# Last stage of a fused two-layer block: one reciprocal root for two norms, bank-wise output copies, earlier signals, filler matmuls and a split store

## The reference

```python
x = x + W_o(softmax(q k^T / sqrt(16)) v)       # L1_xattn over 4096 context rows
x = x + L1_attn(layernorm(x))                  # 16 heads of 64, causal, z.reshape(b, s, h*dh) @ proj
X = layernorm(x)                               # eps 1e-5
nx = X * rsqrt(mean(X*X) + 1e-6) * g1          # RMS norm right behind it
X1 = X + attn(nx Wq, nx Wkc, nx Wvc) @ Wo      # 4 heads, shared keys and values
nx2 = rmsnorm(X1, g2)
logits = nx2 @ Wr.T + expert_bias              # 8 experts, the best two are weighted
moe = swiglu_shared(nx2) + sum_e combine[:, e] * swiglu_e(nx2)
x = x + (X1 + moe)
```

## Time and profile before

| | us |
|---|---|
| median of 3 runs | 748.99 (747.96 to 749.51) |
| the profiled execution | 750.28 |
| its span in the trace | 748.6 |
| PE busy | 646.4 (86%) |
| ACT busy | 464.5 (62%) |
| DVE busy | 413.4 (55%) |
| granted PE clock, mean | 0.963 of full |

### The profile page before, as it was taken

The page is one execution under the profiler, slowest core; times in us unless marked ns, Lnnn a source line. Parts: engine busy times, 40 slices in busy tenths (PEclk is TensorE's granted clock), DMA queues, the critical chain, the costliest instruction groups (busy, mean ns, idle before and its releaser), DMA issues. The chain is left out here.

```text
span 748.6 us, 14468 instructions
## 1 busy us (share of the span) xinstructions
PE 646.4 (86%) x4972; PEld 390.7 (52%) x4972; DVE 413.4 (55%) x903; ACT 464.5 (62%) x558; POOL 71.9 (10%) x148
## 2 busy tenths in 40 slices
PE   1698777878788769898589999999999899988997
PEld 1354444444445345575235555555555567754886
DVE  6576352231322315865578898988883426446443
ACT  3899969999999974472036676767767046303100
POOL 3010201000100003000110101111110200000000
PEclk9999979999999999999758999999999999999899
DMA  5787765384433114000802332323230740000000
GB/s 132 217 245 212 232 205 168 105 239 152 143 112 109 49 25 151 1 1 0 287 9 72 86 81 76 88 79 84 77 83 2 241 139 1 2 0 1 0 1 14
DMA packets 52694, 73.39 MB, mean 98 GB/s; under 512 B 10866, under 2 KB 29618, under 8 KB 52658
## 3 DMA queue, kind: packets, MB, share of 16 engines
q1 hardware_dynamic: 51890, 72.19, 33.0%
q10 hardware_dynamic: 768, 0.73, 0.3%
HBM read 58.89 MB, written 12.85 MB: 96 GB/s over the span
## 5 line engine op out<-in xcount | busy, mean ns | idle before, releaser
L1575 DVE TENSOR_REDUCE sb_m_blk<-ps 128x1 f32<-128x512 f32 x256 | 159.6, 683 | 22.8 <-PE ps L1432 21.7
L1383 ACT ACTIVATE sb_probs<-ps 128x1024 f32<-128x1024 f32 x128 | 125.9, 1025 | 52.9 <-PE ps L1462 51.7
L651 ACT ACTIVATE sb_probs<-ps 128x1024 f32<-128x1024 f32 x128 | 124.0, 1016 | 16.5 <-PE ps L697 14.2
L655 ACT ACTIVATE sb_probs<-sb_probs,sb_neg_cap,sb_cap 128x4096 f32<-128x4096 f32 x32 | 121.6, 3801 | 1.1
L714 PE MATMUL ps<-sb_probs,sb_v_st 128*32 128x256 f32 x1024 | 77.5, 400 | 41.1 <-ACT sb_probs L655 38.7
L1432 PE MATMUL ps<-sb_k_st,sb_q_m 96*128 96x512 bf16 x256 | 91.4, 402 | 2.7 <-DVE sb_m_blk L1575 2.0
L697 PE MATMUL ps<-sb_q_st,sb_k_st 112*128 112x256 bf16 x512 | 76.6, 285 | 5.9 <-DMA sb_k_st<-k_parts_l 4.2
L1462 PE MATMUL ps<-sb_q_st,sb_k_st 115*128 115x256 bf16 x512 | 77.7, 275 | 1.4 <-ACT sb_probs L1383 1.4
L697 PEld LDWEIGHTS ps<-sb_q_st,sb_k_st 112*128 112x128 bf16 x512 | 46.2, 101 | 49.7 <-ACT sb_probs L651 23.8
L1478 PE MATMUL ps<-sb_probs,sb_v_st 128*32 128x256 f32 x1024 | 67.7, 385 | 0.2 <-ACT sb_probs L1383 0.2
L714 PEld LDWEIGHTS ps<-sb_probs,sb_v_st 128*32 128x32 f32 x1024 | 24.2, 110 | 70.4 <-ACT sb_probs L655 49.3
(11 more groups left out here) (264 smaller groups left out, 875.0 us busy)
## 6 DMA issues: line engine op xcount, KB each, us to landing
sb_k_st<-k_parts_l SPq DMA_DIRECT2D x223, 64.0 KB, 2.0
sb_k_st<-k_parts_l SPq DMA_DIRECT2D x93, 128.0 KB, 3.2
k_parts_l<-sb_v_proj SPq DMA_DIRECT2D x24, 256.0 KB
k_parts_l<-sb_early SPq DMA_DIRECT2D x48, 128.0 KB
sb_v_proj<-ctxT_blocks SPq DMA_DIRECT2D x8, 512.0 KB, 8.9
sb_early<-ctxT SPq DMA_DIRECT2D x7, 512.0 KB, 4.0
sb_v_rows<-ctx_by_pair SPq DMA_DIRECT2D x7, 512.0 KB, 3.9
sb_k_st<-k_parts_l SPq DMA_DIRECT2D x64, 32.0 KB, 1.8
```

Of the source, the lines that this page charges most:

```text
L651: a.activation(probs[:, j % 2, 4 * g:4 * g + 4, :], scores_bank(g), ACT.Tanh).then_inc(s["tanh"], 1)
L655: a.activation(probs[:, j % 2], probs[:, j % 2], ACT.Exp, bias=k.neg_cap[:, 0:1], scale=k.cap[:, 0:1]).then_inc(s["exp"], 1)
L1383: sc.activation(probs[:, g], scores_bank(g), ACT.Exp).then_inc(s["exp"], 1)
L1575: v.tensor_reduce(k.m_blk[:, b, q, blk:blk + 1], k.ps[:, m_bank(m_turn_of(idx)), :], AX.X, ALU.max).then_inc(s["m_read"], 1)
```

## The change

- `keep_busy` gets a number of columns; one call of 256 columns (`D`) is added behind the transposes in `update_pe` with `turn=True` (two places), and around the last `sel` of `stage_cross1`.
- `small_dve` calls `beside(n)` at the end of each pair; in the causal attention this copies bank 4, 5 and 6 behind pairs 5, 9 and 13; bank 7 is copied at the end. The first half of the projection waits for two of these copies, the second for all four. The two calls of filler ahead of it are gone.
- The two roots become one ahead of the first use: with variance s of the rows and layer norm scale 1/sqrt(s + 1e-5), the product of both norms' scales is 1/sqrt(s(1 + 1e-6) + 1e-11). `k.xn` is written straight from `k.x`; the layer-normed rows `k.x_ffn` are made later, behind the g1 scaling, with a root of their own. Fillers there go from nine calls to four and one of half width.
- The key product comes first and signals alone, then queries, then values.
- `expert_bias` is loaded to all 128 partitions and added by DVE in place of a copy; the two L1789 products go.
- The last expert's two row tiles go to banks 6 and 7, each with a signal of its own, and `k.x` is stored in two transfers, one for each row tile.

```diff
-    k.f_be = fs[0:1, 1428:1436]
+    k.f_be = fs[:, 1428:1436]
...
+def bn_moments(k, link, src):
 
     v = k.nc.vector
     link(*[v.bn_stats(k.ln_stats[:, t, :], src[:, t, :]) for t in range(QT)])
     link(*[v.bn_aggr(k.ln_mv[:, t, :], k.ln_stats[:, t, :]) for t in range(QT)])
...
-def keep_busy(k, n, bank):
+def keep_busy(k, n, bank, cols=2 * D):
 
     for _ in range(n):
-        k.nc.tensor.matmul(k.ps[:, bank, :], k.ones_sq[:, :], k.w1_o[:, :, :].rearrange("p t n -> p (t n)"), start=True, stop=True)
+        k.nc.tensor.matmul(k.ps[:, bank, 0:cols], k.ones_sq[:, :], k.w1_o[:, :, :].rearrange("p t n -> p (t n)")[:, 0:cols], start=True, stop=True)
...
     if turn:
         transpose_rows(k, k.o_nat, 0, k.sem(tag + "_oT_ps"))
+        keep_busy(k, 1, 3, D)
...
+        if beside is not None:
+            beside(n)
...
+                keep_busy(k, 1, 2, D)
                 sel(H - 1, 1, n_m * H, H - 1)
+                keep_busy(k, 1, 2, D)
...
-    sp.dma_start(k.f_be, i["L1_ffn_expert_bias"].unsqueeze(0)).then_inc(done, 16)
+    sp.dma_start(k.f_be, i["L1_ffn_expert_bias"].unsqueeze(0).to_broadcast([P, N_EXP])).then_inc(done, 16)
...
+    def out_bank(n, q):
+        return 6 + q if n == N_EXP else 4 + n % 2
...
-            sp.wait_ge(k.sem("f_x"), 2 * (N_EXP + 1))
-            sp.dma_start(k.out.rearrange("a (t p) d -> p (a t) d", p=P), k.x[:, :, :]).then_inc(k.sem("out"), 16)
-            sp.wait_ge(k.sem("out"), 16)
+            for q in range(QT):
+                sp.wait_ge(k.sem("f_x"), QT * N_EXP + q + 1)
+                sp.dma_start(k.out.rearrange("a (t p) d -> p (a t) d", p=P)[:, q, :], k.x[:, q, :]).then_inc(k.sem("out"), 16)
+            sp.wait_ge(k.sem("out"), 16 * QT)
...
-            keep_busy(k, 2, 0)
-            pe.wait_ge(k.sem("e_oT"), 1)
-
-
             for q in range(QT):
+                pe.wait_ge(k.sem("e_oT"), 2 * (q + 1))
...
-            keep_busy(k, 9, 0)
+            keep_busy(k, 4, 0)
+            keep_busy(k, 1, 0, D)
...
+            for c in range(KT):
+                last = t.matmul(k.ps[:, 5, 0:S], k.f_wkc[:, c, :], k.xnT[:, c, :], start=(c == 0), stop=(c == KT - 1))
+            last.then_inc(k.sem("f_proj"), 1)
...
-                    t.matmul(o, k.xnT[:, c, q * P:(q + 1) * P], k.f_wr[:, c, :], start=(c == 0), stop=False)
-                last = t.matmul(o, k.ones_row[0:1, 0:P], k.f_be, start=False, stop=True)
+                    last = t.matmul(o, k.xnT[:, c, q * P:(q + 1) * P], k.f_wr[:, c, :], start=(c == 0), stop=(c == KT - 1))
...
+                    if q == 1 or n == N_EXP:
+                        last.then_inc(k.sem("g_rows"), 1)
...
-            v.tensor_copy(k.e_oT.rearrange("p (b g) i c -> p b (g i c)", b=4), k.ps[:, 4:8, :]).then_inc(k.sem("e_oT"), 1)
+            def copy_out(bank):
+                dve.wait_ge(k.sem("small_out"), causal.base + 4 * (bank + 1))
+                v.tensor_copy(k.e_oT.rearrange("p (b g) i c -> p b (g i c)", b=4)[:, bank, :], k.ps[:, 4 + bank, :]).then_inc(k.sem("e_oT"), 1)
+
+            def beside(n):
+                if n % 4 == 1 and n > 4:
+                    copy_out(n // 4 - 1)
+
+            small_dve(k, dve, causal, beside)
+            copy_out(3)
...
-            layer_norm(k, dve, link, k.x, k.x_ffn, k.sem("f_x0"))
-            dve.wait_ge(k.sem("f_x0"), QT)
-            rms_norm(k, dve, link, k.x_ffn, k.sem("f_xn"))
+            bn_moments(k, link, k.x)
+            link(v.tensor_scalar(k.rs_v[:, 0:QT], k.ln_mv[:, :, 1], 1.0 + 1e-6, 1e-5 * 1e-6, ALU.mult, ALU.add))
+            rsqrt(k, link, QT)
+            for q in range(QT):
+                v.tensor_scalar(k.xn[:, q, :], k.x[:, q, :], k.ln_mv[:, q, 0:1], k.rs_y[:, q:q + 1], ALU.subtract, ALU.mult).then_inc(k.sem("f_xn"), 1)
             dve.wait_ge(k.sem("f_w_in"), 16 * 9)
             weigh_turned(k, dve, 0, k.sem("f_xnT_ps"), k.sem("f_xnT"))
-            dve.wait_ge(k.sem("f_proj"), 1)
+            link(v.tensor_scalar(k.rs_v[:, 0:QT], k.ln_mv[:, :, 1], 1e-5, None, ALU.add))
+            rsqrt(k, link, QT)
+            link(*[v.tensor_scalar(k.x_ffn[:, q, :], k.x[:, q, :], k.ln_mv[:, q, 0:1], k.rs_y[:, q:q + 1], ALU.subtract, ALU.mult)
+                   for q in range(QT)])
+            dve.wait_ge(k.sem("f_proj"), 2)
...
+                    if q == 1 and n == N_EXP:
+                        dve.wait_ge(k.sem("g_rows"), n + 2)
```

More of the change, by code:

```diff
@@ L249, in allocate @@
     k.oT_pad = flat(k.v_st[:, :, :, :], "b c n")[:, 0:1024].rearrange("p (g q) -> p g q", g=4)
-def norm_moments(k, link, src):
+def bn_moments(k, link, src):
     v = k.nc.vector
@@ L256, in norm_moments @@
     link(*[v.bn_aggr(k.ln_mv[:, t, :], k.ln_stats[:, t, :]) for t in range(QT)])
+def norm_moments(k, link, src):
+    v = k.nc.vector
+    bn_moments(k, link, src)
     link(v.tensor_scalar(k.rs_v[:, 0:QT], k.ln_mv[:, :, 1], 1e-5, None, ALU.add))
@@ L1057, in small_act, with small_dve @@
     copy_turned(len(a.pairs) - 1)
-def small_dve(k, dve, a):
+def small_dve(k, dve, a, beside=None):
     v = k.nc.vector
@@ L1643, in load_late_weights @@
         sp.dma_start(k.f_g[:, n, :], i[f"L1_ffn_g{n + 1}_cols"]).then_inc(done, 16)
-    sp.dma_start(k.f_be, i["L1_ffn_expert_bias"].unsqueeze(0)).then_inc(done, 16)
+    sp.dma_start(k.f_be, i["L1_ffn_expert_bias"].unsqueeze(0).to_broadcast([P, N_EXP])).then_inc(done, 16)
 def rms_norm(k, dve, link, src, done):
     v = k.nc.vector
-    link(*[v.bn_stats(k.ln_stats[:, t, :], src[:, t, :]) for t in range(QT)])
-    link(*[v.bn_aggr(k.ln_mv[:, t, :], k.ln_stats[:, t, :]) for t in range(QT)])
+    bn_moments(k, link, src)
     link(v.tensor_tensor(k.rs_t[:, 0:QT], k.ln_mv[:, :, 0], k.ln_mv[:, :, 0], ALU.mult))
@@ L1764, in _ @@
             pe.wait_ge(k.sem("f_w_in"), 16 * 9)
+            for c in range(KT):
+                last = t.matmul(k.ps[:, 5, 0:S], k.f_wkc[:, c, :], k.xnT[:, c, :], start=(c == 0), stop=(c == KT - 1))
+            last.then_inc(k.sem("f_proj"), 1)
             for m in range(KT):
                 for c in range(KT):
[L1767 to L1770, removed]
+                    last = t.matmul(k.ps[:, 3, m * S:(m + 1) * S], k.f_wq[:, c, m * P:(m + 1) * P], k.xnT[:, c, :],
+                                    start=(c == 0), stop=(c == KT - 1))
+            last.then_inc(k.sem("f_proj"), 1)
             for m in range(KT):
@@ L1809, in down @@
                     pe.wait_ge(k.sem("f_x"), 2 * (n - 1))
-                rows_linear(k, k.f_hT[:, n % 2], KT, k.f_exp[experts[n]][2], None, 4 + n % 2, k.sem("g_rows"))
+                for q in range(QT):
+                    for c in range(KT):
+                        last = t.matmul(k.ps[:, out_bank(n, q), q * D:(q + 1) * D], k.f_hT[:, n % 2, c, q * P:(q + 1) * P],
+                                        k.f_exp[experts[n]][2][:, c, :], start=(c == 0), stop=(c == KT - 1))
+                    if q == 1 or n == N_EXP:
+                        last.then_inc(k.sem("g_rows"), 1)
             hidden(0)
@@ L1944, in _ @@
                 for q in range(QT):
-                    v.scalar_tensor_tensor(out=k.x[:, q, :], in0=k.ps[:, 4 + n % 2, q * D:(q + 1) * D],
+                    if q == 1 and n == N_EXP:
+                        dve.wait_ge(k.sem("g_rows"), n + 2)
+                    v.scalar_tensor_tensor(out=k.x[:, q, :], in0=k.ps[:, out_bank(n, q), q * D:(q + 1) * D],
                                            scalar=k.f_comb[:, q, experts[n]:experts[n] + 1], in1=k.x[:, q, :],
```

6 lines of the change are left out of this document (3 added, 3 removed).

## The result

| | before | after |
|---|---|---|
| median, us | 748.76 (747.96 to 749.51, 4 runs) | 740.53 (736.70 to 742.25, 4 runs) |
| profiled execution, us | 750.28 | 741.15 |
| span, us | 748.6 | 739.4 |
| granted PE clock, mean | 0.963 | 0.967 |

The ratio is 0.988, 95% interval 0.985 to 0.992: 8.2 us faster, where 9.6 was forecast. In the profiled pair the difference is 9.1 us.

The account below looks back on a forecast made before the run. PE was taken to bound the attention and experts, with latencies between them; gains 1.19 + 3.45 + 0.81 + 0.83 + 1.4 + 1.5 + 0.45 = 9.63 us from 748.99 gave 739.4, own range 738.2 to 741.

Parts of the forecast that it names:

- Copy by bank: Causal attention to projection: 2.42 us gained at the end, 1.23 lost to copies in the loop, net 1.19 (0.35 to 2.1).
- One root: Residual update to transposes in stage_self1: one joint root shortens the path by 3.45 us; the moved DVE work is covered.
- Signals: Latent attention's products to scores: keys, queries and values signalled singly gain 0.81 us (0.4 to 0.85).
- Border fillers: Border ahead of stage_self1: three half-width fillers hold the clock for the output product, gain 1.4 us, other bound 0.
- The router: Router to first expert instructions: a shorter clock dip gains 1.5 us (0 to 3.0), four PE bias instructions fewer gain 0.83.
- bias products: At the router, four PE instructions go as DVE adds the bias: 0.83 us, partly at the low clock.
- the dip lasts half as long: Router's low clock: thin stretch cut from 3.7 to 2.9 us, middle case taken, gain 1.5 us of a 3.0 us cost.
- Store: End of kernel: two transfers, the last issued 0.40 us earlier and landing 0.05 sooner, gain 0.45 us (0.2 to 0.6).
- the clock that doesn't follow: Rival: both dips, at the stage_self1 border and the router, stay; gain 6.73 us, 742.3 us; chance 0.24.
- The clock that follows fully: Rival: router dip vanishes, 737.9 us, or 736.5 with the dip at 280.7 gone too; chance 0.16.
- The copies that eat their gain: Rival in the causal attention: three copies cost 0.69 us each, term 0.35 or below, 740.2 us; inside the forecast's own range.
- The slower one: Rival: shortened fillers let the clock stay low through the latent attention up to the experts, +12 us, 754; chance 0.03.

Follow-up runs that it names:

- One copy: Changed kernel with the four bank copies undone: one copy of 2048 columns behind the causal attention, with filler and one wait as before; median 739.06 us.
- norm alone: Kernel before with only the joint root, the second root behind the g1 scaling and five filler calls for nine; 746.64 us against 749.91, 0.997.
- no border fillers: Changed kernel without its three half-width fillers between stage_cross1 and stage_self1 and the one at the entry of stage_self0; 743.28 us, 0.992 of before.
- even copies: Changed kernel with the bank copies behind pairs 6, 10 and 14 in place of 5, 9 and 13; 737.69 us, 0.986.
- no norm fillers: Changed kernel without the four and a half calls of filler beside the joint norm; 741.91 us.
- stage_cross0 fillers: Changed kernel with two more half-width fillers around the last selection matmul of stage_cross0, and one wait for weights ahead of them; 739.71 us.
- one store: Changed kernel with one transfer of 256 KB behind both updates; the last expert's row tiles keep two banks and a signal each; median 737.84 us.
- control: The changed kernel itself run again on another chip; 738.78 us, 0.986 of 749.93 on that chip.

## Why the prediction was right, and where its sizes were off

**Copy by bank: right.** 1.24 against 1.19. One copy undone gives the 1.24 back, and the copies moved by one pair show that the 1.2 us loss in the loop was wholly the wait of turn(n+1) behind the copy. Copy by copy it measured 0.55, 0.55 and 0.10. The upper bound, none of the copies covered, and the lower, hidden slack in a PE that looked full, were both wide of it.

**One root: right.** 3.44 against 3.45, and 3.43 when done alone. The moved 2.26 us of DVE is covered with either order of signals.

**Signals: right**, 0.81. It is seen in the kernels with the new order and signals; the run with the norm alone kept 4.87. The two were not tried one without the other.

**Border fillers: right in mechanism, cautious in size.** Product to addition took 2.11 in all eleven traces of kernels with these fillers, and 3.49, 3.90 and 3.49 in the three without (before, norm alone, changed kernel without them). The eleven began the product anywhere from 581.4 to 587.5 us, the three at 584.7 to 585.7, so its place in time is no rival. The value is 1.4 where the dip would be single and 2.9 in the one trace where it was double. The one filler at the entry of stage_self0 did not hold the clock in the changed kernel's trace, as assumed. The prediction's bound of 1.4 for that place was too high: by the traces a shorter product gains nothing there, since DVE gets on only at the end of POOL's fill.

**The router: sizes right, the case by luck.** Forecast 1.5 of dip and 0.83 for the bias products; the ledger has 1.29 and 1.11, together 2.40 against 2.33. They divide otherwise: at the full clock logits to first expert instruction took 1.71 us with the bias products and 0.91 without, so these are worth 0.80, and the other 0.31 of that line is dip, since in the trace of before the last logits ran at the low clock. The dip term is then 1.60. But "the dip lasts half as long" is not what the change does, and that the profile showed just this case is luck. There are eight traces with the changed router and no filler there. The dip came in four (changed kernel, no border fillers, even copies, no norm fillers), with 8.67 to 8.68, and not in the other four (one copy, stage_cross0 fillers, one store, control), with 6.99. With a filler it was absent in all three traces, which at a chance of one half would happen once in eight, so that the filler holds the clock is likely and not shown. The kernels with the bias products had it in all three: 9.97, 10.02, 8.70. The right statement is a chance of a dip and its cost: 1.7 us for one of the single length (8.68 - 6.99), 3.3 for a double one, logits included (9.97 - 6.99 + 0.31).

**Store: mis-sized.** Forecast 0.40 + 0.05, measured 0.39 + 0.44. The step that failed is the landing: 2.0 us for 64 KB was taken from loads of the attention, a median among other traffic, and set beside a lone store. A lone store of 128 KB lands in 1.7, of 256 KB in 2.2. Even a straight line between the two rows used would have given 0.13 and not 0.05. The Trainium skill ("DMA: Bandwidth & Descriptors", "Anatomy of one DMA") has a fit for transfers that GpSimd issues, 2.0 us and the bytes at 436 GB/s. As an estimate from it, 256 KB would take 2.6 us and 128 KB 2.3. The stores here, which SP issues, land sooner than both and differ by 0.44 and not 0.3; the measurement decides.

**What the sum left out.** Ahead of the border the changed kernel was 0.97 us later. The change didn't do this: its profile is 0.6 us behind at 29 us, ahead of any dip, and 1.09 behind at 112 us, where both kernels have run the same instructions. Both show the same six dips ahead of the border, each as long in one as in the other and 0.8 to 0.9 us later in the changed kernel. At 535 us it is 0.90 behind, so neither the filler in stage_self0 nor the broadcast load of the bias costs anything on the way. What makes the first 1.1 us stays open. In the other profiles with the changed code the border's output product began anywhere from 581.4 to 587.5 us, and there the dips do differ in time and length, between 34 and 42, 93 and 108, 273 and 297, and 364 and 399 us. A median of four such runs is uncertain by 1 to 2 us (an estimate from their range of 5.6).

For the profiled execution the forecast was 740.65 and the measurement 741.15: 0.97 late ahead of the border, 0.48 more gained behind it. The rest of the error of 1.4 in the gain is in the medians: the changed kernel's lies 0.6 under its profiled execution where the prediction took 1.3 from the kernel before, and the median of before moved from 748.99 to 748.76 with a fourth run. The gain of the first measurement (8.2) and that of the control (11.2) stand on both sides of the 9.6, so that the forecast median came within 1.1 us of the measured one is partly luck.

The rivals: the clock that doesn't follow is out for the border; at the router the dip came in half of the traces without a filler. The clock that follows fully would have gained nothing from the dip at 280.7 us. The copies that eat their gain did eat half of it, as forecast. The slower one was tested without any cover and cost 2.0 us.

## What to carry to other kernels

In a loop that two engines share, look for the side of the period on which the helper engine waits before putting work on it: the same copy cost 0.55 us behind an odd pair and nothing behind an even one. Compare small edits stretch by stretch in traces, since whole times may spread by more than the edits are worth, and give a clock dip as a chance and a price. Before filling a thin place, look at what ends last behind it: at the entry of stage_self0 a product 1.8 us shorter gained nothing. Take a landing time from a transfer in the same surroundings, direction and load included.

## What the runs showed of the hardware that was not expected

- Where the clock falls differs from run to run of nearly the same code. From 270 to 300 us the low clock came at 281.6 to 285.0 in the changed kernel's first profile, 276.0 to 282.9 in the second, and in two places in the run with fillers at the end of stage_cross0.
- A dip that came in the last stage lasted about 3.4 us or about twice that (6.8), and a single length at 1.2 GHz cost 1.4 us on the border's chain and 1.7 on the experts'. Over the output product at the entry of stage_self0 it cost nothing.
- Two wide PE instructions in a wait of 1.0 us at the router (0.86 us of work) cost nothing at all on the path, and no dip came behind them in either trace.
- While POOL filled `k_st` (6.92 us), DVE's addition and its `bn_stats` ran at their usual lengths (0.69 us, and 0.75 for two), but a `tensor_scalar` on 128x2, 0.17 us in stage_self1, ended only with the fill, up to 2.68 us after its start. So it was in all fourteen traces.
- A store of 128 KB at the end of the kernel landed 0.44 us sooner than one of 256 KB.
